# Three clearings of semaphores joined to the next one, edge increments and waits of TensorE moved to their first use, GpSimd's block additions cut into tiles

## The reference

```
x = x + attn_a(layernorm(x))   # 2 layers of: retention (8 heads of 32, decay mask, group
                               #   norm, silu gate) + residual, then a feed-forward part:
                               #   silu(LN(y) @ w1 + b1) @ w2 + b2 + y, 1024 hidden
x = x + ffn(layernorm(x))      # ternary weights, rms norms, gelu, 1024 hidden
x = x + attn_b(layernorm(x))   # 16 query and 4 key heads of 16, window of 64, rotary, softmax
x = x + ffn(layernorm(x))
```

## Time and profile before

| | |
|---|---|
| median of 3 runs | 1516.62 us (1515.74 to 1516.77) |
| the profiled execution | 1518.72 us, its span 1516.9 us |
| TensorE busy | 1443.2 us, 95% |
| VectorE, ScalarE, GpSimd busy | 69%, 62%, 53% |
| mean granted TensorE clock | 0.988 |

### The profile page before, as it was taken

How to read it: one execution, slowest core, us unless ns; L and a number is a source line. 1 busy time by engine, 2 the same in 40 slices (tenths; PEclk the granted TensorE clock), 3 DMA queues, 4 the chain that set the end, 5 groups by cost and what they waited for, 6 DMA issues and landing times. The chain is left out here.

```text
span 1516.9 us, 36350 instructions
## 1 busy us (share of the span) xinstructions
PE 1443.2 (95%) x13066; PEld 1196.5 (79%) x13066; DVE 1046.7 (69%) x2272; ACT 936.7 (62%) x1760; POOL 809.2 (53%) x843
## 2 busy tenths in 40 slices
PE   4999999899998999999999999997999999989998
PEld 3777777799996788887899988886777777768886
DVE  4777877565446887785755668775777777756775
ACT  5556555465554545545655567775777777757775
POOL 2566676312013666663523257775666666636674
PEclk9999999999999999999999999999999999999999
DMA  7000000100001000000300010000000000000011
GB/s 247 2 2 2 0 2 2 35 1 1 1 1 56 2 2 0 1 2 1 125 29 15 1 40 1 0 1 2 2 1 0 0 0 0 0 2 1 31 41 42
DMA packets 21095, 26.27 MB, mean 17 GB/s; under 512 B 1904, under 2 KB 19056, under 8 KB 20848
## 3 DMA queue, kind: packets, MB, share of 16 engines
q1 hardware_dynamic: 18432, 21.64, 4.3%
q10 hardware_dynamic: 2544, 3.04, 0.6%
HBM read 20.48 MB, written 4.19 MB: 16 GB/s over the span
## 5 line engine op out<-in xcount | busy, mean ns | idle before, releaser
L543 DVE TENSOR_TENSOR ffn_h_lo<-ffn_h,ffn_h_hi 128x512 fp32r<-128x512 f32 x112 | 94.0, 841 | 116.1 <-ACT ffn_h_hi L750 116.0
L749 ACT ACTIVATE ffn_h<-ffn_hp,c_b 128x512 f32<-128x512 f32 x112 | 77.2, 689 | 153.2 <-PE ffn_hp L846 152.7
L543 DVE TENSOR_TENSOR ternary_ffn_h_lo<-ternary_ffn_h,ternary_ffn_h_hi 128x512 fp32r<-128x512 f32 x128 | 110.0, 860 | 75.0 <-ACT ternary_ffn_h_hi L750 74.8
L1187 POOL TENSOR_TENSOR ret_qk<-ret_qk,ret_qk_sin 128x512 f32<-128x512 f32 x64 | 82.6, 1291 | 103.2 <-DVE ret_qk_sin L1284 102.7
L857 PE MATMUL ternary_ffn_yp<-down_ternary,ternary_ffn_h_hi 128*128 128x256 f32 x512 | 132.6, 291 | 0.0
L857 PE MATMUL ffn_yp<-down_hi,ffn_h_hi 128*128 128x256 f32 x448 | 127.7, 285 | 0.9 <-DVE ffn_h_lo L543 0.9
L857 PE MATMUL ternary_ffn_yp<-down_ternary,ternary_ffn_h_lo 128*128 128x256 f32 x512 | 127.6, 281 | 0.0
L1193 POOL TENSOR_TENSOR ret_rstd<-ret_sums,ret_minus_half 128x16 f32<-128x16 f32 x32 | 103.7, 3240 | 42.9 <-DVE ret_sums L1326 42.9
L857 PE MATMUL ffn_yp<-down_hi,ffn_h_lo 128*128 128x256 f32 x448 | 125.2, 279 | 0.0
L857 PE MATMUL ffn_yp<-down_lo,ffn_h_hi 128*128 128x256 f32 x448 | 125.2, 279 | 0.0
L2081 POOL TENSOR_TENSOR win_rms<-win_rms,win_minus_half 128x20 f32<-128x20 f32 x31 | 115.2, 3716 | 2.6
(11 more groups left out here) (315 smaller groups left out, 4786.5 us busy)
## 6 DMA issues: line engine op xcount, KB each, us to landing
X<-in_x SPq DMA_DIRECT2D x8, 512.0 KB, 10.1
staging<-in_w SPq DMA_DIRECT2D x4, 1024.0 KB, 8.5
ffn_x_in<-in_x SPq DMA_DIRECT2D x8, 512.0 KB, 3.9
out<-X SPq DMA_DIRECT2D x7, 512.0 KB, 2.9
rotary<-in_rotary ACTq DMA_DIRECT2D x1, 1024.0 KB, 7.6
staging<-in_w_up SPq DMA_DIRECT2D x1, 1024.0 KB, 4.9
staging<-in_w_down SPq DMA_DIRECT2D x1, 1024.0 KB, 7.5
staging<-in_wqkv ACTq DMA_DIRECT2D x1, 768.0 KB, 5.9
```

The lines of the kernel that those rows point to most:

```text
L543: nc.vector.tensor_tensor(h_lo[:, m % R, :], h[:, m % R, :], h_hi[:, m % R, :].bitcast(F32), ALU.subtract).then_inc(h_ready, 1)
L749: nc.scalar.activation(h[:, m % R, :], hp[m % 2][:, :], fn, bias=bias)
L1187: nc.gpsimd.tensor_tensor(qk[:, r, :, :, :], qk[:, r, :, :, :], qk_sin[:, r, :, :, :], ALU.add).then_inc(qk_done, 1)
```

## The change

Six edits. (1) The `with nc.cleanup_on_exit()` ahead of `ffn` in the layer loop and ahead of `window_attention` are gone, so that `ret0`+`ffn0`, `ret1`+`ffn1` and `ternary_ffn0`+`wa` share one clearing each, at the end of the pair. The barrier at the end of each stage's block stays. (2) In `ffn`, PE's increments move behind the first hidden slice that it makes. (3) In `ffn`, PE's wait for GpSimd's memsets moves to the first sum of squares, the first that reads them; in `retention`, PE's wait for `consts_set` moves to the first `chunk_out`, and its increment behind the first projection. (4) In `window_attention`, PE's increments move to pass n = 3, and VectorE's are put in another order. (5) In `retention`, VectorE raises `xt_ready` first. (6) `add_constants` works tile by tile: four operations of 128x256 for one of 128x1024, the semaphore raised by the last.

```diff
                 if first_input is not None:
                     pool.wait_ge(in_loaded[k % 2], 16 * (i + k // 2 + 1))
                     apart(pool, pool_waited)
-                    nc.gpsimd.tensor_tensor(blk, blk, x_in[:, k % 2, :, :], ALU.add).then_inc(bias_in, 1)
+                    for t in range(TB):
+                        last = nc.gpsimd.tensor_tensor(blk[:, t, :], blk[:, t, :], x_in[:, k % 2, t, :], ALU.add)
+                    last.then_inc(bias_in, 1)
                     pool.wait_ge(bias_in, b + 1)
                 apart(pool, pool_waited)
-                nc.gpsimd.tensor_tensor(blk, blk, out_bias[:, :].unsqueeze(1).to_broadcast([P, TB, D]),
-                                        ALU.add).then_inc(added, 1)
+                for t in range(TB):
+                    last = nc.gpsimd.tensor_tensor(blk[:, t, :], blk[:, t, :], out_bias[:, :], ALU.add)
+                last.then_inc(added, 1)
...
                 if half == 0:
                     at_least(pe, ms_done, b)
+                    if at_start(b):
+                        pe.wait_ge(powers_set, 4)
...
-            if ternary:
-                pe.wait_ge(powers_set, 4)
-            if ready:
-                pe.sem_inc(tp_full, KD * BEGUN)
-            if begun:
-                pe.sem_inc(h_full, MF)
-                pe.sem_inc(h_used, MF - 1)
-                pe.sem_inc(y_full, 2)
+            def made_before():
+
+                if ready:
+                    pe.sem_inc(tp_full, KD * BEGUN)
+                if begun:
+                    pe.sem_inc(h_full, MF)
+                    pe.sem_inc(h_used, MF - 1)
+                    pe.sem_inc(y_full, 2)
...
                         if to_do(b):
                             up_product(b, m, k)
+                        if m == 0 and isinstance(g, int) and g == 1 + BEGUN:
+                            made_before()
...
             if first is None:
+                dve.sem_inc(xt_ready, KD)
                 dve.sem_inc(stats_done, TB)
                 dve.sem_inc(mv_done, 1)
-                dve.sem_inc(xt_ready, KD)
...
                 t, par = at % TB, at // TB % 2
+                if at_start(n):
+                    pe.wait_ge(consts_set, 3)
                 pe.wait_ge(pr_done, n + 1)
...
-            pe.wait_ge(consts_set, 3)
             if first is not None:
                 pe.wait_ge(early_loaded, 16 * len(first["early"]))
-            else:
-                pe.sem_inc(tp_full, KD)
...
                         project_heads(n, b, k - AHEAD)
+                    if at_start(n) and first is None:
+                        pe.sem_inc(tp_full, KD)
...
+            dve.sem_inc(padded_done, 1)
+            dve.sem_inc(xt_ready, TB)
+            for ready in (sq_sum_done, rot_done, rot_sum_done):
+                dve.sem_inc(ready, 1)
+            for ready in (stats_done, mv_done, xn_done):
+                dve.sem_inc(ready, TB)
             dve.sem_inc(yt_ready, C0)
             dve.sem_inc(wo_done, C0)
-            for ready in (stats_done, mv_done, xn_done, xt_ready):
-                dve.sem_inc(ready, TB)
-            for ready in (sq_sum_done, rot_done, rot_sum_done, padded_done):
-                dve.sem_inc(ready, 1)
...
-            pe.sem_inc(wo_full, C0)
-            pe.sem_inc(yt_full, C0)
-            pe.sem_inc(tp_full, TB)
-            pe.sem_inc(qkv_full, 2)
+            def made_before():
+
+                pe.sem_inc(qkv_full, 2)
+                pe.sem_inc(wo_full, C0)
+                pe.sem_inc(yt_full, C0)
+                pe.sem_inc(tp_full, TB)
...
                         transpose_queries(n - 3, k - 3)
+                    if isinstance(n, int) and n == 3:
+                        made_before()
...
                               first=None if layer else dict(x=d["x"], early=early, weights=ret_stages[0], tables=tables,
                                                             halves=ret_halves[0], values=values[0]), **tabs)
-                with nc.cleanup_on_exit():
                     ffn(nc, f"ffn{layer}", X, ident, lane, up=up, down=down, norm=kept["ln2"][:, layer],
...
-        with nc.cleanup_on_exit():
             window_attention(nc, "wa", X, ident, lane, qkv=win_qkv, out_w=win_out, gain=gain,
```

## The result

| | before | after |
|---|---|---|
| median, same chip | 1516.39 us (1513.99 to 1518.23, 9 runs) | 1511.56 us (1510.55 to 1513.26, 9 runs) |
| ratio, 95% interval | | 0.9969 (0.9961 to 0.9978) |
| profiled execution, its span | 1518.72, 1516.9 | 1512.02, 1510.2 |

The change makes the kernel 4.8 us faster. That is inside the range of 1510.5 to 1518.5, but 3 us under the sum, in the case of "faster by over 0.2%" that had a chance of 0.36. The two profiled executions lie 6.7 us apart, more than the medians (4.8), so some of what the two traces show is chance; the repeated profiles further down separate it out.

A forecast was written before the change was run, and what follows sets the result against it. TensorE, busy 95% of the span, was taken as the bound. Clearings -1.35, ffn0 -2.0, ffn1 +0.4, ternary stages -0.6 and half clocks +0.85 and +0.8 summed to -1.9 us: 1516.62 to 1514.7 us, range 1510.5 to 1518.5.

The forecast's parts named there:

- the sum: Whole kernel: all terms together give -1.9 us, a median of 1514.7 us.
- faster by over 0.2%: Whole kernel: the outcome of a gain above 3.0 us, needing 1513.6 us; chance 0.36.
- Clearings: Stage edges: joining clearings removes 2.5 us, of which 1.16 come back in longer clears; net -1.35 us.
- Nothing left over: Joined clears: a range clear costs 6 ns a semaphore, so clearing two stages takes as long as two clears.
- Edges: Six edges between stages: joined clearings, TensorE's earlier starts in ffn0, ffn1, ret1 and wa, and -0.6 in the ternary stages.
- ret1 and wa give theirs back: TensorE starts 1.15 us earlier in ret1, 0.75 in wa, but later waits for inputs make both worth 0.
- each of four xn operations waits for a tile and takes its own 0.33, less 0.1 of overlap: 4 x 0.95: Start of ffn0 and ffn1: VectorE's four xn operations among GpSimd's tiles take 3.8 us.
- hardly cost anything since xn was late anyhow: Start of ffn0: the existing half-clock stretch at 288.8 costs almost nothing, because TensorE waits for xn anyway.
- ffn1: xn is used at 748.6 instead of 748.21, so TensorE loses its earlier start: +0.4 us net.
- Rival (a): ffn0 and ffn1: tiles are cheap (0.62) and no half clock follows; -5.5 us, 1511.1 us; chance 0.33.
- Rival (b): ffn0 and ffn1: VectorE does not get in between tiles; about 0 overall, 1516.7 us; chance 0.12.
- Rival (c): Tiles ahead of xn in ffn1 and ffn0 cost 0.90 or more; slower, +3.0 at 0.90, +5.6 at 1.0; chance 0.12.

The follow-up runs named there:

- e3: The kernel before with only the three clearings joined: 1514.06 us, ratio 0.9987 to the kernel before.
- e9: The changed kernel with GpSimd's additions in halves (two of 128x512) in place of tiles: 1515.18 us, ratio 0.9991 to the kernel before.
- e4: The changed kernel with block 3's scale made ahead of the additions to blocks 0 and 1 in ffn0 and ffn1: 1508.24 us, ratio 0.9942.
- e6: The changed kernel, unchanged, run and profiled again: 1511.97 us, ratio 0.9968 to the kernel before.
- e12: The changed kernel with TensorE's increments in ffn put back ahead of its first matmul: 1513.94 us, ratio 0.998 to the kernel before.
- e11: The kernel of e8 with TensorE's wait for the memsets and its increment put back to the start of ret1: 1505.22 us, ratio 0.9925.
- e2: The kernel before with GpSimd's additions by tile and nothing else: 1514.01 us, ratio 0.9986 to the kernel before.
- e5: The kernel before, unchanged, run again for a second profile: 1516.99 us in a single run.
- e1: The changed kernel with GpSimd's additions whole again (128x1024), so only the edges are changed: 1516.59 us, ratio 1.0000 to the kernel before.
- the second pair: Repeat profiles of the kernel before (e5) and the changed kernel (e6), both unchanged: spans 1515.2 and 1510.6 us.
- e8: The kernel of e4 with VectorE's wait for the memsets in ret1 moved ahead of its first operation on the state: 1504.03 us, ratio 0.9925.
- e10: The kernel of e4 with GpSimd's additions whole again: 1511.41 us, ratio 0.9966 to the kernel before.

## Why the prediction was right in range and short in size

**Clearings: right.** Predicted -1.35; e3 measured 0.9987. That is 2.0 us, with an interval from 0.6 to 3.5; in its trace the six edges are 1.8 shorter and the end 0.5 longer. The joint clears of the two pairs of retention and ffn differ by the 48 ns that the single ones differed by. "Nothing left over" was wrong: joining two clears saves 42 ns.

**Edges: right.** The terms for the six edges add up to -5.1 (-2.5 + 1.16 for the clearings, -1.3, -1.15 and -0.75 for what TensorE starts earlier in ffn0 and ffn1, ret1 and wa, -0.6 for the ternary stages); measured -5.5. Nothing came due in TensorE's sequencer for the moved increments.

**ret1 and wa give theirs back: right.** Predicted inside ret1 +1.15 for the wait and +0.8 for a half clock; measured +1.9 and +2.6 in the two pairs. Over all profiles with the early start and a wait over 2 us, six of seven have a second stretch of half clock in ret1 (e9 has not; in e4 it is joined to the first), and none of the five with a wait of 1.0. That the wait draws it is not shown: in e6 and e12 it begins only behind the next wait, and e11 has it there with no such wait before. In wa +0.75 was predicted, +0.8 and +0.9 measured.

**Where it failed, first: the step "each of four xn operations waits for a tile and takes its own 0.33, less 0.1 of overlap: 4 x 0.95".** It measured 0.75 in every kernel with tiles (3.04 over four). The tile with an xn operation behind it lasts 0.77 to 0.79, against 0.73 without, so letting one in costs GpSimd 0.05 us, not the 0.43 of a 128x512 subtraction with two inputs, and VectorE's own time overlaps the tile's start. That is 0.8 us too much in ffn0 and 0.8 in ffn1. In ffn1 what led up to it held: the scale stood at 23.6, where the text had 743.2 - 719.6 = 23.6, and a tile from start to start was 0.70.

In ffn0 it came out by luck. xn began 5.2 us behind the barrier, where the text had 4.2 + 0.7 + 0.45 = 5.35, but by another way: the scale was there at 4.8, since its last operation took 1.56 us beside a subtraction and not 1.04, and xn then started right behind a subtraction that no tile had held up. With a half clock at the stage's start xn does not begin at 5.35: e2 has the text's 4.2 for the scale, and its xn begins at 7.3. What the text left out is the wait of the second subtraction for TensorE's second slice.

**Second: the clock in ffn0.** The text let the half clock at 288.8 stand as something that "hardly cost anything since xn was late anyhow" and added +0.85 for a new one. In its place the runs showed that the old stretch goes when the edge is short. All five profiles with an edge of 1.79 to 2.67 ahead of ffn0 have it (before, e5, e2, e3, e12), none of the nine at 1.18 or 1.19 has. What decides it is not shown: in all nine TensorE's increments are moved too, and ffn1's start never had the stretch. And it had cost something, by way of that second subtraction: xn stands behind it, so a slower or later TensorE makes its own xn later. e2 and e12 show the price: 165.9 and 166.0 in ffn0 for 164.5. The new stretch did come in e1, where the wait is 3.04, did not in e9, where it is 2.82, and did not where tiles cut it to 0.62. The prediction gave TensorE's increments no worth of their own beyond xn's time; e12 puts them at about 1.8 us, with overlapping intervals. Inside ffn0 the prediction's terms come to -0.5 us (1.35 gained, 0.85 lost to the new stretch), and -2.4 was measured; this is the largest part of what the sum was short by.

**ffn1.** Predicted inside the stage +1.05 (0.65 given back and 0.4 for xn), measured -1.5 in the first pair and -0.2 in the second. The 0.8 of xn explains most of the way to -0.2; the other 1.4 is the stretch that comes or not in the same kernel. A reader of the first two traces alone would have put it down to the change.

**The rivals.** Rival (a), 1511.1 us, gave the right time for a partly wrong reason: the half clock did not follow in ffn0, but tiles in a row were no cheaper than 0.70, only those with xn between them were cheaper than forecast, and ret1, where rival (a) had nothing for a half clock, got one. Rival (b), that nothing gets in between tiles, is out. The GPSIMD Engine Reference of the Trainium skill (Instruction dispatch) lets the next instruction start before the last is complete; here VectorE got in behind every one of the tiles it was waiting for. The Trainium skill's SBUF — State Buffer (SBUF: two separate sides) calls the pair of ports that the two engines share an exclusive lock for the whole instruction. The traces agree, with 1.31 us for an xn operation behind a half and 2.9 for a subtraction behind a whole addition; one instruction of GpSimd, and no more, is what VectorE sat out. Rival (c), a tile of 0.90 or more, did not occur.

The terms as they were: edges -5.5, ffn0 -2.4, ret1 +1.9 to +2.6, ffn1 -0.2 (or -1.5 with luck), ternary_ffn0 -0.5, wa +0.9, the end +0.5. No term of the prediction stood for the last one nor for ternary_ffn0. In the second pair, with ret0's -0.4 and +0.4 at the start and in ternary_ffn1, that is -4.6 in the span, beside -4.8 between the medians.

## What to carry to other kernels

When one engine's start is moved forward, ask who makes its next input and what stands ahead of that in the maker's queue: the gain is kept only if that input moves too (e1: 5.5 us of edges and nothing in the time; e8: one wait moved off the statistics, and ratio 0.9925 against e4's 0.9942, with overlapping intervals). Put the short operation that others wait for ahead of a backlog, and cut the backlog too. By the ratios, the cut alone brought 4.7 us (e1 to the changed kernel), the order alone 5.2 (e1 to e10), and either on top of the other 3.6 to 4.1 more (e4). A stretch of half clock that differs between two traces is only a result once a second profile of each kernel shows it too.

## What the runs showed of the hardware

- How much GpSimd loses to a VectorE operation that gets in depends on that operation: 0.05 us for the 128x256 tensor-scalar with one input, 0.43 to 0.51 for the 128x512 subtraction of two. Statistics (L515, 0.41 us) ran beside tiles at their own length.
- The same wait of about 2 us was followed by half clock in six of ten profiles in ffn1, and in ret0 the stretches near 33 us differ from profile to profile (268.4 to 271.2 us for the same work). The two profiles of the changed kernel, with and without it in ffn1, put a stretch at 1.4 us there, and runs of one kernel differ by 2 to 6; that these are the cause is likely, not shown, as only one run of each has a profile.
- The start of ffn1, with an edge as long as ffn0's (2.62), never had the stretch of half clock that ffn0's start had every time at 2.67. Why is open.
- From the last matmul to the end of the span it takes 7.2 us in the three profiles without joined clearings and 7.7 in all eleven others, e3 and the changed kernel's two among them. From the issue of the last store to the end of SyncE's wait for it, it takes 2.2 us in the first profile before and 2.7 in the first after. No run tried what causes it; it stays open.
